# Row statistics of three layer norms: from VectorE's statistics instructions to ScalarE's row sums and squared distances

## The reference, cut to what matters

```python
def _layernorm(x, axis=-1, eps=1e-05):
    m = jnp.mean(x, axis=axis, keepdims=True)
    v = jnp.var(x, axis=axis, keepdims=True)
    return (x - m) / jnp.sqrt(v + eps)
...
    x = x + 0.5 * ffn(_layernorm(x), W_r, W_k, W_v, mu_r, mu_k)
    x = x + attn(_layernorm(x), ln_w, ln_b, W_in, W_conv, ...)   # a Mamba block: its own norm inside
    x = x + 0.5 * ffn(_layernorm(x), W_r, W_k, W_v, mu_r, mu_k)
```

## Time and profile before

| | before |
|---|---|
| median of 3 runs | 4893.64 us (4893.16 to 4895.35) |
| the profiled execution | 4890.04 us, span 4888.0 |
| VectorE (DVE) busy | 4488.3 us, 92% |
| TensorE (PE) busy | 4296.9 us, 88% |
| GpSimd (POOL) busy | 3196.4 us, 65% |
| ScalarE (ACT) busy | 2900.1 us, 59% |
| chain that ended last | DVE 38%, PE 29%, issue 16%, ACT 7%, POOL 6% |

### The profile page before, as it was taken

One profiled execution on the slowest core, in us unless ns is written; L12 is line 12 of the kernel. 1 busy time (PEld: TensorE's weight loads), 2 busy tenths in 40 slices (PEclk: granted clock), 3 DMA queues, 4 the chain that ended last, 5 costly groups with the idle time before them and its releaser, 6 DMA issues.

```text
span 4888.0 us, 58099 instructions
## 1 busy us (share of the span) xinstructions
PE 4296.9 (88%) x16896; PEld 2382.9 (49%) x16896; DVE 4488.3 (92%) x3650; ACT 2900.1 (59%) x6355; POOL 3196.4 (65%) x3328
## 2 busy tenths in 40 slices
PE   6777989898999989989898899989999898999787
PEld 2444545454554545545454454545545454554443
DVE  2799999999999999999999999999999999999992
ACT  2555656666666566656666665666656666665452
POOL 1666767576676767767576676767667576776770
PEclk9888999999999999999999999999999999999798
DMA  2445555454554555555555554555555565655451
GB/s 82 141 135 180 172 171 185 163 183 162 189 169 151 189 168 186 172 173 185 158 174 163 186 172 152 190 179 176 172 185 173 155 180 156 190 170 153 167 164 62
DMA packets 423053, 810.71 MB, mean 166 GB/s; under 512 B 41264, under 2 KB 41264, under 8 KB 418640
## 3 DMA queue, kind: packets, MB, share of 16 engines
q1 hardware_dynamic: 422736, 807.00, 52.1%
HBM read 772.25 MB, written 34.60 MB: 165 GB/s over the span
## 4 chain that ended last, share of the span: by engine, by line
DVE 38%; PE 29%; issue 16%; ACT 7%; POOL 6%; DMA 3%; DVEq 0%; SPq 0%; POOLq 0%; ACTq 0%
DVE decay L1091 19%; DVE g L1099 10%; PE y_acc L567 6%; PE mm L494 5%; PE mm L483 5%; POOL dbx L1298 4%; PE mm L472 4%; DVE xc L1037 3%; DMA c_all<-bc_scratch 2%; PE mm L531 2%; PE mm L509 2%; PE mm L519 2%; DVE xc L1043 1%; ACT decay L889 1%; POOL xout L1287 1%
## 5 line engine op out<-in xcount | busy, mean ns | idle before, releaser
L1298 POOL TENSOR_TENSOR dbx<-u,b_all 128x1024 f32<-128x1024 f32 x1024 | 2414.2, 2358 | 902.6 <-DVE g L1099 901.7
L1091 DVE TENSOR_TENSOR_SCAN decay<-decay,state,dbx 128x1024 f32<-128x1024 f32 x1024 | 2405.4, 2349 | 172.4 <-ACT decay L889 157.6
L567 PE MATMUL y_acc<-ident,g 128*128 128x128 f32 x8192 | 1124.2, 283 | 372.5 <-DVE g L1099 370.6
L567 PEld LDWEIGHTS y_acc<-ident,g 128*128 128x128 f32 x8192 | 947.4, 144 | 939.1 <-DVE g L1099 713.2
L1099 DVE TENSOR_TENSOR g<-decay,c_all 128x1024 f32<-128x1024 f32 x1024 | 1244.3, 1215 | 10.0 <-DMA c_all<-bc_scratch 1.1
L886 ACT ACTIVATE decay<-delta,neg_a 128x512 f32<-128x512 f32 x1024 | 708.7, 692 | 36.9
L889 ACT ACTIVATE decay<-delta,neg_a 128x511 f32<-128x511 f32 x1024 | 686.9, 671 | 0.0
L895 ACT ACTIVATE state<-decay 128x2 f32<-128x2 f32 x1024 | 166.9, 163 | 508.6 <-DVE g L1099 506.1
L494 PE MATMUL mm<-wbuf_c,col 128*128 128x512 f32 x1024 | 460.9, 594 | 2.1 <-ACT col L758 1.3
L1037 DVE SCALAR_TENSOR_TENSOR xc<-mm,conv_sb,xc 128x509 f32<-128x509 f32 (+2 forms) x384 | 285.3, 743 | 47.0 <-ACT xs_last L804 35.7
L1302 POOL TENSOR_TENSOR dbx<-dbx,carry 128x1 f32<-128x1 f32 x1024 | 274.2, 268 | 80.3
(11 more groups left out here) (100 smaller groups left out, 5107.4 us busy)
## 6 DMA issues: line engine op xcount, KB each, us to landing
b_all<-bc_scratch SPq DMA_DIRECT2D x1024, 256.0 KB, 3.4
c_all<-bc_scratch SPq DMA_DIRECT2D x1024, 256.0 KB, 3.6
wbuf_d<-in_w_r SPq DMA_DIRECT2D x32, 1024.0 KB, 7.5
wbuf_c<-in_w_v SPq DMA_DIRECT2D x32, 1024.0 KB, 7.3
xin<-in_x SPq DMA_DIRECT2D x16, 1024.0 KB, 6.8
wbuf_c<-in_w_k SPq DMA_DIRECT2D x16, 1024.0 KB, 6.7
wbuf_d<-in_w_in SPq DMA_DIRECT2D x16, 1024.0 KB, 5.8
wbuf_a<-in_w_in SPq DMA_DIRECT2D x16, 1024.0 KB, 8.0
```

The lines of the kernel that those rows point to most:

```text
L567: last = pe.matmul(y_acc[:, tb, j * P:(j + 1) * P], g[:, s % PAIRS, j, tb * P:(tb + 1) * P], ident[:, :], start=n == 0 and j == 0 and tb % ...
L1091: dve.tensor_tensor_scan(d, d, flat(dbx[:, s % DBX, :, :]), state[:, batch, s, 0:1], ALU.mult, ALU.add).then_inc(scan_done, 1)
L1298: pool.tensor_tensor(dbx[:, s % DBX, :, :], u[:, q % 2, :, :], b_all[:, s % BRING, :].unsqueeze(1).broadcast_to([P, QT, W]), ALU.mult).the ...
```

## The change

VectorE's statistics and aggregates are removed. ScalarE instead makes, for each tile of 128 rows, a row sum (a Copy activation with `accum_out`), then `minus` = -sum/512 for four tiles at once, and then the row sum of (x - mean)^2 (a Square activation with bias `minus` and `accum_out`). For norm 1 the row sums come out of VectorE's `out_add` instead. GpSimd takes the variance as sum/512, and the negation of `shift` falls away, since `minus` is negative already. The tables of steps change in a few places.

```diff
-        stats = [sb(f"stats{i}", [P, TB, 6]) for i in range(3)]
-        mv = [sb(f"mv{i}", [P, TB, 2]) for i in range(3)]
+        total = [sb(f"total{i}", [P, TB]) for i in range(3)]
+        minus = [sb(f"minus{i}", [P, TB]) for i in range(3)]
+        square = [sb(f"square{i}", [P, TB]) for i in range(3)]
+        dump = sb("dump", [P, D])
...
-        SUM_SKIP = (5, 27, 35, 53)
+        SUM_SKIP = (5, 25, 35, 53)
-        XS = (28, 30, 34, 36, 38, 40, 43, 46)
+        XS = (28, 29, 34, 36, 38, 40, 43, 46)
-        ZEROS = {2: 2, 31: 2, 39: 2, 30: 1, 53: 1}
+        ZEROS = {2: 2, 31: 2, 39: 2, 30: 1, 53: 1, 52: 1}
-        NORM = ((58, 58, 58, 58), (31, 31, 31, 31))
+        NORM = ((61, 61, 61, 62), (31, 31, 31, 31))
-        CTANH = (30, 32, 37, 38, 40, 42, 45, 48)
-        XROWS = 51
+        CTANH = (31, 32, 37, 38, 40, 42, 45, 48)
+        XROWS = 52
-        STATS = ((51, 53, 53, 54), (9, 22, 24, 27), (18, 19, 20, 21))
-        MEANS = (56, 27, 21)
-        FFN_ADD = ((18, 19, 20, 22), (57, 58, 59, 60))
-        RSTD = (58, 30, 24)
-        HISTORY = 26
-        ADD_HEAD = (32, 34, 38, 40, 42, 44, 47, 50)
+        FFN_ADD = ((18, 18, 19, 21), (57, 58, 59, 60))
+        RSTD = (60, 31, 24)
+        HISTORY = 27
+        ADD_HEAD = (31, 34, 38, 40, 42, 44, 47, 50)
-  (LOAD)  "bc_out": 52
+  (LOAD)  "bc_out": 53
+        SUMS = ((50, 50, 52, 52), (26, 26, 26, 26), (17, 18, 20, 21))
+        SQUARES = ((55, 56, 57, 58), (27, 28, 29, 29), (21, 22, 22, 23))
...
+            def row_sum(i, k, tb):
+                if i == 1:
+                    act.wait_ge(y_dve.sem, y_dve.at(k, f"x{TB - 1}"))
+                else:
...
+                    if i == 2:
+                        act.wait_ge(f_pool[0].sem, f_pool[0].at(k, f"o{tb}"))
+                    act.activation(rows[0][:, tb, :], xin[:, tb, :], ACT.Copy,
+                                   accum_out=total[i][:, tb:tb + 1]).then_inc(s_act[i].sem, 1)
+                    if tb == TB - 1:
+                        act.wait_ge(s_act[i].sem, s_act[i].at(k, f"su{tb}"))
+                if tb == TB - 1:
+                    act.activation(minus[i][:, :], total[i][:, :], ACT.Copy, scale=-1.0 / D).then_inc(s_act[i].sem, 1)
+            def row_squares(i, k, tb):
+                act.wait_ge(s_act[i].sem, s_act[i].at(k, f"sq{tb - 1}" if i == 1 and tb else "minus"))
+                act.activation(dump[:, :] if i == 1 else rows[0][:, tb, :], (xout if i == 1 else xin)[:, tb, :], ACT.Square,
+                               bias=minus[i][:, tb:tb + 1],
+                               accum_out=square[i][:, tb:tb + 1]).then_inc(s_act[i].sem, 1)
...
(ScalarE, body: behind skip_columns, ahead of mamba_inner)
+                    if front:
+                        for n in at(SUMS[2], s):
+                            row_sum(2, f, n)
+                        for n in at(SQUARES[2], s):
+                            row_squares(2, f, n)
+   (then the same for norm 1 of b, and for norm 0 of it + 2)
...
-                                         op0=ALU.mult, op1=ALU.add).then_inc(y_dve.sem, 1)
+                                         op0=ALU.mult, op1=ALU.add,
+                                         accum_out=total[1][:, tb:tb + 1]).then_inc(y_dve.sem, 1)
...
-                pool.wait_ge(f_dve[i].sem, f_dve[i].at(k, "mv3"))
+                pool.wait_ge(s_act[i].sem, s_act[i].at(k, "sq3"))
-                pool.tensor_scalar(nv[i][:, 0:TB], mv[i][:, :, 1], 1.0, EPS, ALU.mult,
+                pool.tensor_scalar(nv[i][:, 0:TB], square[i][:, :], 1.0 / D, EPS, ALU.mult,
-                pool.tensor_tensor(shift[i][:, 0:TB], mv[i][:, :, 0], rs[i][:, 0:TB],
+                pool.tensor_tensor(shift[i][:, 0:TB], minus[i][:, :], rs[i][:, 0:TB],
-                pool.tensor_scalar(shift[i][:, 0:TB], shift[i][:, 0:TB], -1.0, 0.0, ALU.mult,
-                                   ALU.add).then_inc(f_pool[i].sem, 1)
```

More of the change, by code:

```diff
@@ L213, in build @@
                      *[(GATE[i][n], f"g{n}") for n in range(4)])) for i in range(2)]
-        f_pool = [Marks(sem(f"ffn{i}_pool"), ["v"] + newton + ["mean", "shift", "o0", "o1", "o2", "o3"])
+        s_act = [Marks(sem(f"sums{i}_act"), in_order(*[(SUMS[i][n], f"su{n}") for n in range(4 if i != 1 else 0)], (SUMS[i][3], "minus"),
+                                                     *[(SQUARES[i][n], f"sq{n}") for n in range(4)])) for i in range(3)]
+        f_pool = [Marks(sem(f"ffn{i}_pool"), ["v"] + newton + ["mean", "o0", "o1", "o2", "o3"])
                   for i in range(2)]
@@ L977, in body @@
                     if front:
+                        for n in at(SUMS[2], s):
+                            row_sum(2, f, n)
+                        for n in at(SQUARES[2], s):
+                            row_squares(2, f, n)
+                    if back:
+                        for n in at(SUMS[1], s):
+                            row_sum(1, b, n)
+                        for n in at(SQUARES[1], s):
+                            row_squares(1, b, n)
+                    if ahead:
+                        for n in at(SUMS[0], s):
+                            row_sum(0, it + 2, n)
+                        for n in at(SQUARES[0], s):
+                            row_squares(0, it + 2, n)
+                    if front:
                         for n in at(INNER, s):
@@ L1148, in body @@
                             conv_taps(f, e)
-                        for n in at(STATS[2], s):
-                            inner_stats(f, n)
-                        if s == MEANS[2]:
-                            row_means(2, m_dve, f)
-                    if ahead:
-                        for n in at(STATS[0], s):
-                            in_stats(it + 2, n)
-                        if s == MEANS[0]:
-                            row_means(0, f_dve[0], it + 2)
-                    if back and s == MEANS[1]:
-                        row_means(1, f_dve[1], b)
                     if scn:
```

58 lines of the change are left out of this document (16 added, 42 removed).

## The result

The changed kernel takes 4905.61 us (median of 12 runs, 4899.76 to 4912.03) where the kernel before, on the same chip in turns, takes 4892.82 (12 runs, 4889.3 to 4895.35): a ratio of 1.0025, 95% interval 1.0017 to 1.0033. That is 12.8 us slower, a little over what this kernel's measurement can tell. The forecast was 4892 and no measurable change. Two things stand out beside the median: the runs of the changed kernel lie 12 us apart, twice as far as the 12 of the kernel before, and the profiled execution, at 4899.76 us (span 4897.4), is the fastest of the 12. All that is read from its trace explains 9.4 us of span, not 12.8.

The account below looks back on a forecast made before the run. VectorE and TensorE were taken to bound the kernel by turns, so VectorE savings count only in its own stretches. Chunks -22 and start and end +20.5 gave -1.5 us against 4893.64, so 4892, range 4874 to 4918.

Parts of the forecast that it names:

- slower: Whole kernel: the changed kernel takes measurably longer, 4914 us in the case worked out; chance 0.31.
- no measurable change: Whole kernel: the time, 4892 us, differs by under 0.2% (9.8 us); the forecast, chance 0.42.
- the chunk's gain: Steps 18 to 32: 1.5 at scan 25, 0.95 for step 27's removed statistics, 0.3 at scan 32, together 2.75 us earlier.
- 2 us later than before, still a step ahead of need: GpSimd behind the second norm's root: products 25, 26 and the head history come 2 us later without delaying anything.
- Scan 25: After the second norm's chain on ScalarE and GpSimd: the scan starts at 2297.8 instead of 2299.33, 1.5 us earlier.
- Steps 50 to 60: Removed statistics (2.8 us, steps 51 to 56), later `x_rows`: no effect; added zero product at 52: nothing, at most 1.3 us.
- free of cost inside a TensorE stretch: Kernel before, scan 59: the normalization at 58 held it 0.60 us, at no cost to the total.
- The normalization at 61: Three of four rows at step 61 (before 58) make scan 62 1.13 us late, counting in full.
- Start and end: Norms everybody waits for, at the run's start and end, and a later first scan: together +20.5 us.
- The second norm's chain takes all: Steps 20 to 25: row sums 0.17 us dearer, scan 25 gains nothing, 4914 us; chance 0.31.
- No stall at 61: Scan 62 has unseen room, so 14 x 1.13 = 16 us go: 4876 us; chance 0.23.
- VectorE's whole load counts: Whole kernel: all 135 us taken off VectorE shorten the time, to 4779 us; chance 0.04.

Follow-up runs that it names:

- e1: Changed kernel with only the 1 MB transfer `res_out` issued at step 27 instead of 26, behind the load of c for step 29: 4881.88 us.
- e13: Kernel before, all statistics still on VectorE, with the new steps alone (`res_out` at 27, norm 0's rows at 61, 62, 62, 62, no zeros at 52): 4851.87 us.
- e11: e5 without the product with zeros that the change adds on TensorE at step 52: 4833.97 us.
- e5: Changed kernel with `res_out` at 27, norm 2's fourth square at 22, norm 0's rows at 61, 62, 62, 62, and the start put in order: 4846.55 us.
- e3: Changed kernel with norm 0's four normalization rows at steps 61, 62, 62, 62 instead of 61, 61, 61, 62: 4887.95 us.
- e4: Changed kernel with all sums and squares of the second chunk's norm 0 at step 50, ahead of the first chunk: 4893.08 us.
- e9: e5 with norm 0's statistics back on VectorE: 4844.18 us.
- e10: e5 with norm 2's statistics (the second norm, Mamba's) back on VectorE: 4847.01 us.

## Why the prediction was wrong

The time, 4905.6, lies inside the stated range (4874 to 4918) but not where the forecast stood: slower had a chance of 0.31, no measurable change 0.42.

**The step that failed** is the chunk's gain, "1.5 + 0.95 + 0.3 = 2.75 us earlier at scan 32", and in it the sentence that GpSimd's products come "2 us later than before, still a step ahead of need". The 2 us were right (2.3), and the products were in time (each of products 23 to 32 was ready 1.6 us or more before its scan in chunks 1 to 13). What stands behind them was not followed: SyncE's queue, where the load of c for step 29 comes after a load that waits for product 28. That load had 1.7 to 3.2 us to spare before. In its place stood a wait in each of 15 chunks of the profiled execution (25.4 us in all, 1.7 in the mean). e1 takes only that away, and scan 32 comes 2.66 us earlier, where 2.75 was predicted. So the sum up to there was right but for one missing term, worth 23.7 us by the medians, more than the whole miss of 13.6: without it the chunks gain 28.2 us from first scan to last (e1), where 22 were predicted. The single terms were right only in the sum. In e1 scan 25 comes 1.40 us earlier (1.5 predicted), scans 25 to 30 give 0.52 (0.95 predicted) and scans 30 to 32 give 0.74 (0.3 predicted). The last is a gift of the new steps, which alone give 1.03 there (e13) and were taken at nothing but for the wait of 0.3 at scan 32.

**Scan 25**: right, 1.46 against 1.5, partly by luck. The row sums cost 0.61 and 0.70 us and not 0.79 and 0.87, 1.0 us less for the six of the chain. A wait of 0.48 for VectorE inside the chain and a root of 5.5 us instead of 5.0 took about that back, and the root's last operation ended at 101.9 us into the chunk (2306.92 - 2205.05), where 101.5 was worked out (2293.2 - 2191.71).

**Steps 50 to 60 "worth nothing"**: the sum was right to scan 55 (1.32 to 1.24 us), the reason incomplete. Two terms cancel: `x_rows` one step later with its companions gives 0.8 us (e13), the product of zeros takes 0.87 (e11). Its bound, at most 1.3, held. From scan 55 to 59 the chunk gained another 1.0 us that the prediction had not counted: the aggregates at 56 (0.26) and norm 0's rows, which no longer hold scan 59 (0.71). The prediction had called that old wait "free of cost inside a TensorE stretch", and for the greater part it was: in e5, which has no stall at 61, 0.6 of the 1.0 is gone again by scan 62 and 0.4 reaches the next chunk (in e13 0.3 of 0.7).

**The normalization at 61**: right in place and size, 1.15 us measured in the wait against 1.13, and it counted in full (e3). The chunk loses 1.86 us between scans 59 and 62; the rest is the gain at scan 59 that is given back.

**Start and end**: +18.6 (15.2 and 3.4) against +20.5. The mechanism was the one described, root ahead of `make_u` behind squares; the squares were quicker than taken (the eight instructions and the scaling of norm 0 run from 14.10 to 19.85, 5.7 us against 6.9). e4 shows that 11 us of it were a matter of order alone.

**The measured quantities**: VectorE's busy time fell by 108 us, not 120 to 135. The first scan was at 168.78, just below 170 to 175. The middle chunks followed each other 0.4 us closer and not 1.5. `mamba_inner` waited for GpSimd, as forecast (2.50 us in this chunk), and the wait of 1.15 before scan 62 was there.

**The rivals.** "The second norm's chain takes all" was nearest in time (4914 against 4905.6) with a wrong mechanism: row sums are cheaper than taken, not dearer. "No stall at 61" falls. "VectorE's whole load counts" falls most clearly: 108 us went from VectorE, and of the three norms two give nothing when moved (e9, e10). The rule of the Trainium skill, "Perfetto Trace Analysis", section "Identifying the Most-Contended Engine", to optimize the engine of highest occupancy first, misleads in this case: VectorE is the busiest at 92%, and of the statistics taken from it only norm 1's are worth something, 1.4 us per chunk, in the one place where VectorE waits for nobody.

## What to carry to other kernels

When an edit makes one engine's work later by a microsecond or two, follow every in-order queue behind it to its end, transfers too, and ask for each how much time it had to spare; a wait of zero in the profile before says nothing of that margin, which is landing time against the start of the reader. An engine that is made faster eats into the same margin from the other side: here 1.9 us of it. Where such a load shares its queue with large transfers whose readers are far off, putting them behind it costs nothing and gives the margin back (23.7 us here). And before crediting a change of engine with a gain, run the new order without it: here two thirds of the 58 us won in the end lay in the steps (39.9), a third in one norm of three (18.4).
